# A decoder layer on one core: the context load split into 112 and 13 partitions, and batch 0's context parts released earlier

## The reference

```python
x = layernorm(x + attn(x))          # causal, 16 heads of 32, projected by Wu
q = x @ Wq.T + bq                   # cross attention, one head of 512
k, v = ctx @ Wk.T + bk, ctx @ Wv.T + bv
x = layernorm(x + softmax(q @ k.T) @ v)
# a gated recurrence over the 16 sequences; c has shape (224, 512)
c = sigmoid(xt @ wf.T + c @ uf.T + bf) * c + sigmoid(xt @ wi.T + c @ ui.T + bi) * tanh(xt @ wc.T + c @ uc.T + bc)
x = layernorm(x + tanh(x @ wo.T + c_final @ uo.T + bo))
```

## Time and profile before

| | |
|---|---|
| median of 3 runs | 1415.11 us (1411.97 to 1417.11) |
| the profiled execution, its own time | 1416.02 us |
| its span in the trace | 1414.1 us |
| TensorE busy | 98% of the span |
| mean granted TensorE clock | 0.994 |

### The profile page before, as it was taken

How to read it: one execution, slowest core, us unless ns; L and a number is a source line. 1 busy time by engine, 2 the same in 40 slices (tenths; PEclk the granted TensorE clock), 3 DMA queues, 4 the chain that set the end, 5 groups by cost and what they waited for, 6 DMA issues and landing times.

```text
span 1414.1 us, 28483 instructions
## 1 busy us (share of the span) xinstructions
PE 1385.4 (98%) x10017; PEld 1211.0 (86%) x10017; DVE 921.9 (65%) x1911; ACT 731.6 (52%) x1989; POOL 569.7 (40%) x475
## 2 busy tenths in 40 slices
PE   7999999999999999999999999999999999999997
PEld 4677777777789999999999988999999999999775
DVE  4589989999657756776677663345453444536697
ACT  4488888888565566656665655222232222222232
POOL 2476767676476565656565620000000000010264
PEclk9999999999999999999999999999999999999999
DMA  7014323335366675667567953010010100000353
GB/s 212 25 56 107 104 75 81 104 104 156 109 172 215 200 240 182 204 195 233 188 205 213 210 155 112 1 27 13 13 26 0 26 13 19 31 1 31 101 186 123
DMA packets 133079, 157.94 MB, mean 112 GB/s; under 512 B 62304, under 2 KB 70496, under 8 KB 133008
## 3 DMA queue, kind: packets, MB, share of 16 engines
q1 hardware_dynamic: 133008, 157.01, 37.8%
HBM read 105.61 MB, written 35.78 MB: 100 GB/s over the span
## 4 chain that ended last, share of the span: by engine, by line
PE 64%; issue 3%; POOL 3%; DMA 1%; DVE 1%; ACT 1%; POOLq 0%; ACTq 0%; DVEq 0%
PE banks L1522 16%; PE banks L1551 11%; PE banks L1007 9%; PE banks L1023 8%; PE banks L1036 6%; PE banks L1553 6%; PE banks L992 5%; POOL o_r L2097 1%; PE banks L977 1%; DMA s_cx_raw<-in_cx 1%; PE banks L1983 1%; PE banks L1053 1%; POOL o_rstd L2105 1%; POOL x_cx_lo L1367 1%; PE banks L2014 0%
## 5 line engine op out<-in xcount | busy, mean ns | idle before, releaser
L461 ACT ACTIVATE s_p<-banks,a_nmax 112x224 f32<-112x224 f32 (+1 forms) x512 | 198.1, 412 | 60.0 <-DVE a_nmax L572 59.9
L759 POOL TENSOR_TENSOR s_p<-s_p,a_rinv 112x896 f32<-112x896 f32 (+1 forms) x128 | 164.5, 1306 | 118.9 <-DVE a_rinv L580 115.8
L1496 POOL CAST m_hi<-w_raw 128x2048 fp32r<-128x2048 f32 x1 | 2.3, 2266 | 407.8 <-PE banks L1522 407.8
L1639 ACT ACTIVATE f_gate<-f_gate 128x448 f32<-128x448 f32 x90 | 52.2, 580 | 198.6 <-DVE f_gate L1762 198.6
L1759 DVE TENSOR_TENSOR f_gate<-banks,f_xg_early 128x448 f32<-128x448 f32 x45 | 28.1, 624 | 189.6 <-PE banks L1553 189.6
L1367 POOL TENSOR_TENSOR x_cx_lo<-s_cx_raw,x_cx_hi 125x512 fp32r<-125x512 f32 x96 | 120.8, 1296 | 37.0 <-ACT x_cx_hi L1136 37.0
L571 DVE TENSOR_REDUCE a_nmax<-banks 112x1 f32<-112x224 f32 x256 | 97.9, 382 | 24.5 <-PE banks L277 23.7
L461 ACT ACTIVATION_READ_ACCUMULATOR s_p<-banks,a_nmax 112x1 f32 x512 | 111.6, 218 | 0.0
L294 PEld LDWEIGHTS banks<-identity,s_p 112*112 112x112 f32 x768 | 88.0, 134 | 21.8 <-issue 2.3
L294 PE MATMUL banks<-identity,s_p 112*112 112x112 f32 x768 | 105.4, 261 | 1.2 <-POOL s_p L759 0.7
L1360 POOL TENSOR_TENSOR s_ct<-s_ct_raw,s_ct 128x750 fp32r<-128x750 f32 x60 | 98.6, 1669 | 0.0
(11 more groups left out here) (255 smaller groups left out, 3727.5 us busy)
## 6 DMA issues: line engine op xcount, KB each, us to landing
s_ct_raw<-in_ct SPq DMA_DIRECT2D x16, 1500.0 KB, 6.7
s_cx_raw<-in_cx SPq DMA_DIRECT2D x16, 1500.0 KB
a_xt<-in_xt SPq DMA_DIRECT2D x16, 448.0 KB, 6.3
a_xrow<-in_x SPq DMA_DIRECT2D x16, 448.0 KB, 5.9
a_xres<-in_x SPq DMA_DIRECT2D x16, 448.0 KB, 6.7
x_scratch<-a_xn SPq DMA_DIRECT2D x16, 448.0 KB, 3.3
x_scratch<-x_xn SPq DMA_DIRECT2D x16, 448.0 KB, 4.6
x_halves<-x_halves SPq DMA_DIRECT2D x16, 448.0 KB, 3.2
```

Source lines behind the costliest of these rows:

```text
L461: e = act.activation((p1 if c else p0)[:, g, h, :], src, ACT.Exp, bias=nmax[:, g % 2, c, h:h + 1], accum_out=rsum[:, g % 2, c, h:h + 1])
L759: pool.tensor_tensor(p[:, g, :, :], p[:, g, :, :], inv, ALU.mult).then_inc(norm_done, 1)
```

## The change

The context rows are loaded by a new function in two DMAs, of partitions 0 to 111 and 112 to 124, for all 16 batches. Both count up the same semaphore, and `cxh` waits for 32 a batch in place of 16. At the joint, ACT and POOL wait for the last residual (`r_done`) in place of the last norm (`xn_done`). POOL's first step does `cxl(0)` first, then waits for the last norm, and then does `residual_bias(0)`; ACT waits for the last norm just before `exp(0)`, behind `cxh(0)`.

```diff
-            sp.dma_start(shared.cx_raw[:], io["cx"][0].rearrange("(c p) d -> p c d", p=XR)).then_inc(shared.cx_in, 16)
+            shared.load_context(sp, 0)
...
-                sp.dma_start(cx_raw[:], io["cx"][b].rearrange("(c p) d -> p c d", p=XR)).then_inc(cx_in, 16)
+                shared.load_context(sp, b)
...
             def cxh(b):
-                wait(act, cx_in, 16 * (b + 1))
+                wait(act, cx_in, 32 * (b + 1))
...
             def exp(b):
+                if isinstance(b, int) and b == 0:
+                    act.wait_ge(shared.xn_done, TC * B)
...
             x1th(1)
-            act.wait_ge(shared.xn_done, TC * B)
+            act.wait_ge(shared.r_done, TC * B)
...
         def gpsimd(pool):
-            pool.wait_ge(shared.xn_done, TC * B)
+            pool.wait_ge(shared.r_done, TC * B)
...
             def step(i, odd):
                 b = 2 * i + odd
+                if isinstance(b, int) and b == 0:
+                    cxl(0)
+                    pool.wait_ge(shared.xn_done, TC * B)
+                    residual_bias(0, 0)
+                    return
                 if within(b, B):
                     residual_bias(i, odd)
-                    if not (isinstance(b, int) and b == 0):
-                        ctl(b)
+                    ctl(b)
...
+            def load_context(sp, b):
+
+                rows = io["cx"][b].rearrange("(c p) d -> p c d", p=XR)
+                for part in (slice(0, R), slice(R, XR)):
+                    sp.dma_start(cx_raw[part], rows[part]).then_inc(shared.cx_in, 16)
+
+            shared.load_context = load_context
```

More of the change, by code:

```diff
@@ L2167 @@
     xn_done: object
+    load_context: object = None
 @dataclass
```

## The result

| | before | after |
|---|---|---|
| median of 7 runs each, alternating on one chip | 1417.11 us (1411.97 to 1420.59) | 1409.64 us (1408.46 to 1411.59) |
| the profiled execution, its own time | 1416.02 us | 1409.47 us |
| its span | 1414.1 us | 1407.5 us |
| mean granted TensorE clock | 0.994 | 0.997 |

The ratio is 0.9952, with a 95% interval of 0.993 to 0.9973. The change makes the kernel faster by about 0.45%, some 6.5 us.

What follows compares the result with a forecast made beforehand. TensorE, always busy in batches 2 to 14, bounds the kernel; only joint idle time can give. -1.46 - 2.07 - 0.94 + 1.8 = -2.7 us, giving 1412.4 us, no measurable change; range 1408.8 to 1418.5, likeliest case 1410.5 to 1414.5.

Steps and rivals of the forecast that it cites:

- Where the change acts: Joint of two stages only: three TensorE idle places, together 5.00 us; batches 2 to 14 keep 28.5 us each.
- First idle place: TensorE before the projection at 362.07: context load spread wide, store lands sooner, -1.46 us; bounds -1.99 and 0.
- Batch 1's load: TensorE before `zt` of batch 2 at 422.67: context lands sooner, wait goes, -2.07 us; bounds -2.07 and -1.0.
- SyncE's issue: Batch 1's context load, behind x's rows for batch 2: issued at about 394 instead of 395.4, counted as nothing.
- Scores of batch 1: TensorE at 405.28: POOL's new order ends `ctl(1)` sooner, idle place goes, -0.94 us; other bound +2.5 us.
- a late `ztl(1)`: Before batch 1's scores: VectorE's row-bias operations held until POOL is through push the scores to 407.6, a +2.5 us bound.
- The norms under GpSimd's run: VectorE's last two norms, asked at 384.36 under POOL's run, delay TensorE's transposes: +1.8 us, with +0.45 and +5.5 kept.
- passed over once between them: VectorE's last two norms miss one instruction end of POOL, are through at 388.8, transposes at 393.8: +1.8 us.
- I count 0 for the clock: Behind the first idle place, 363.7: granted clock could stay up; counted as 0, with 1.7 us kept as bound.
- The clock stays up as well: Rival, at 363.7: forecast plus 1.7 us of clock, -4.4 us, 1410.7 us; chance 0.15.
- POOL shuts the norms out: Slow rival, at the joint: port kept all run, last norm done at 392.4; +1.0 us, 1416.1 us; chance 0.3.
- The early store changes nothing: Rival, at the norm at 359.96: its store is late anyway; sum -1.2 us, 1413.9 us; chance 0.1.

Runs made afterwards that it cites:

- the order alone: Kernel after, with the context loaded by one DMA of 125 partitions, against the kernel before: 1.0022 [1.0009, 1.0034], median 1419.56 us.
- second profile of before: Profile from measuring the kernel before once more with no edit, against itself: 1.0001 [0.999, 1.0013], median 1417.01 us.

## Why the prediction was right, and where it wasn't

The places and the three gains were right, and three things put the time outside the likeliest case: the cost of the norms, the fall of the clock counted as nothing, and other executions of the kernel before, which lose time where the one that was read doesn't. The whole range held the time. But by the forecast's own measure (what can be told from no change is 0.3%, 4.2 us) the gain of 6.5 us is a real one, and it had given such a gain a chance of 0.14.

**Where the change acts.** Right. The joint is all of it; batches 2 to 14 stay at 375.00 of 375.00 us.

**First idle place, -1.46.** Right: 1.53 measured, by the mechanism told. With only batch 0's load unsplit the gap is 1.65 us, with only that load split it is 0.45. In the three kernels with the new order and this load in one DMA it is 1.25 to 1.65 us, not 1.99; what takes off the difference isn't shown. (By the forecast's own figures the DMA of 13 partitions goes over 13 engines, not all 16; nothing hangs on it.)

**Batch 1's load, -2.07.** Right in place and size: 2.36 in the profiles, no gap left. In time the split is worth more, 6.5 to 7 us between the kernel after and the one with only batch 0 split. Part of it is that under the new order the undivided load lands later (next point).

**SyncE's issue, "nothing beside 16.58 us".** The issue moved as forecast, by 0.96 us against batch 0's transposes, where 1.4 was told. What the forecast left out is that the load's own length changes: undivided, it takes 19.35 and 18.90 us under the new order and lands 1.8 and 1.4 us later against the same transposes, which with the issue behind the rows of x turns a gain into a loss: 1.0022 for the order alone. The forecast had costed the move as part of a sum in which the split was already there, and never asked what the order would be worth by itself.

**Scores of batch 1, -0.94.** Right: -1.10 in the profiles. The bound on the other side, a late `ztl(1)`, was real, but in the kernel before and in the one with the swap without early release (2.64 and 3.33 us), not in the one after. With the swapped order the early release is needed, as far as one profile and the time of that kernel (0.9981) show.

**The norms under GpSimd's run, +1.8.** The term that was mis-sized: +0.16 in the profiles. The step that failed is "passed over once between them". The first norm took 1.20 us and the second 1.51: each got in at the next end, the case for which I had kept +0.45. (By its own numbers, POOL's ends would be at 385.2 and 386.45 and the norms through at about 387.0, not 387.5, so that case was nearly free.) The chain behind the norms was right, and is tight: the chain that ended last in the kernel after runs from the last norm through the low part of x, the row maximum and both exponentials into the transposes. The last norm ends at 382.95 and the transposes begin at 388.18, 5.23 us later, where the forecast had 5.0; all nine profiles with the early release have these 5.23 us.

```profile
381.44 1.51 DVE a_xn L624
...
384.01 0.86 DVE x_smax L1254
...
387.15 0.98 ACT x_p L1152 x2
388.14 0.04 issue
388.18 1.56 PE banks L977 x12
```

The slack was in the kernel before, where the transposes began at 392.05, 6.69 us behind the last norm's end at 385.36. ScalarE had `cxh(0)` to do until 388.55, though the first row maximum had ended at 387.27:

```profile
386.34 0.93 DVE L1252 TENSOR_REDUCE x_smax<-banks 112x1 f32<-112x750 f32 x1
```

```profile
388.55 0.28 ACT L1144 ACTIVATE x_biased_max<-x_smax,s_rowbias 112x1 f32<-112x1 f32 x1
```

And the second exponential waited 0.21 us more for the second row maximum, which waits for TensorE's scores and not for the norms. With `cxh(0)` moved ahead of the norms this 1.3 us is gone from ScalarE's list, and so 0.16 of the 1.63 us that the norms lose reach TensorE.

**"I count 0 for the clock".** The second term that was mis-sized. The fall behind the first idle place is in both profiles of the kernel before (gaps of 1.99 and 2.02 us) and in that of no other kernel, also not in the three with batch 0's load in one DMA, whose gaps there were 1.25, 1.32 and 1.65 us. So it goes with the longer gap as far as these profiles show, one execution for each kernel, and the rival *The clock stays up as well* (1410.7 us) is nearest to the 1409.64 measured. Between the two profiles only 0.63 of its 1.7 us are kept, since the 0.92 us gap stands behind it without the fall. In the second profile of before, with both fall and gap, the stretch from one projection to the next takes 10.73 us, where it takes 9.84 in the first and 9.21 in the kernel after: there the fall costs 1.52 us. The forecast took a single trace of before as its typical run, and a second one had a longer gap and a second, longer fall.

**The sum.** -1.53 - 2.36 - 1.10 + 0.16 - 0.63 = -5.46, and +0.78 behind `zt` of batch 2: -4.68. Of the +0.78, 0.37 are there by batch 2's transposes and 0.27 come in the stages behind cross attention; what makes them isn't shown. The two wrong terms are 2.3 us of the miss, and the clock over many runs is about 2 us more.

**The other rivals.** *POOL shuts the norms out* didn't happen to the norms. The rule of the Trainium skill (SBUF — State Buffer, Who interferes with whom), the holder of the port pair blocks the other for its whole instruction, fits the norms and doesn't cover the dot products, which were passed over at several ends (8.01, 9.03, 9.27 us). By that rule the sum was about -4.0 us, nearer to what came than mine, -2.7. *The early store changes nothing* fell with the store's 5.7 us.

**Open.** Why a held VectorE operation gets in at the next end of GpSimd's run in some cases and at none in others. How the 2 us beyond the equal-clock difference divide among executions. Why one undivided load takes 16.58 us and another 19.35. The 6.5 to 7 us for batch 1's split and the 5.9 us of its profile are not told apart by these intervals.

## What to carry to other kernels

Look at the shape of every large load: one of 125 partitions held a third of the DMA engines and made a small store behind it late, and TensorE stood behind it. When an edit has two parts, work out each alone: here one was all of the gain that the runs resolve, and the other, alone, a loss. Where an edit makes one engine late, ask what the same edit frees on the next one in the chain: here that paid for nearly all of the norms' loss. And before a term is built on one profile of a kernel whose runs spread over 0.6%, ask whether the waits that it shows are the ones of every run.

## What the hardware showed that I had not expected

- Dot products of VectorE held for 7.7 to 9.3 us, passed over at up to four ends in GpSimd's back-to-back run, where one takes 0.68 us with GpSimd idle (L662 at 363.88 after, the same shape). Others in such a run got in at the next end (2.83 us in the kernel before at 395.97).
- One and the same load of 125 partitions took 16.58 us in the kernel before, and 19.35, 18.90 and 18.1 us in three kernels with the new order. The columns and the transposed x were issued 9.8 to 9.9 us behind it before and in the first two alike; what differs there is that the rows of x were issued 0.37 us ahead of it, in place of 7.46. No run isolates that.
- The kernel before's time follows its mean clock, 1418.47 us at 0.993 and 1414.24 at 0.997, and the clock differs between runs of one binary.
